# Forty series of five matmuls on one Trainium2 core behind the last product of a graph layer: weights from other tiles and at other strides, moving columns in other orders

## The reference, cut to what matters

```python
h = maximum(layernorm(x, axis=-1), 0.0)      # x: (4096, 256)
agg = matmul(adj, h)                         # adj: (4096, 4096)
out = x + relu(matmul(agg, W.T) + b)         # W: (256, 256), b: (256,)
```

## Time and profile before

| | us |
|---|---|
| device time, median of 2 runs | 382.73 (382.58 to 382.88) |
| device time of the profiled execution | 382.79 |
| span of the profiled execution, first to last instruction | 381.0 |
| TensorE busy with matmuls | 376.3 (99%) of 1649 matmuls |
| TensorE loading weights | 308.2 (81%), 1649 loads |
| DVE, ACT, POOL busy | 218.1, 170.9, 63.0 |

### The profile page before, as it was taken

How to read it: one execution, slowest core, us unless ns; L and a number is a source line. 1 busy time by engine, 2 the same in 40 slices (tenths; PEclk the granted TensorE clock), 3 DMA queues, 4 the chain that set the end, 5 groups by cost and what they waited for, 6 DMA issues and landing times.

```text
span 381.0 us, 4425 instructions
## 1 busy us (share of the span) xinstructions
PE 376.3 (99%) x1649; PEld 308.2 (81%) x1649; DVE 218.1 (57%) x293; ACT 170.9 (45%) x197; POOL 63.0 (17%) x79
## 2 busy tenths in 40 slices
PE   8999999999999999999999999999999999999996
PEld 4888888888888888888888888888888888888885
DVE  5999999994745353535564535353565344444424
ACT  4656655654553434343644343434364334343414
POOL 2787777760010000000001000000000100000000
PEclk9999999999999999999999999999999999999999
DMA  7987778669649565656565856565657675656203
GB/s 235 372 288 263 261 267 268 209 201 321 204 156 348 175 214 175 209 179 209 175 207 184 312 178 210 177 211 173 212 174 209 239 255 181 210 181 205 68 2 110
DMA packets 23062, 80.25 MB, mean 211 GB/s; under 512 B 2496, under 2 KB 3264, under 8 KB 23040
## 3 DMA queue, kind: packets, MB, share of 16 engines
q1 hardware_dynamic: 21024, 72.36, 58.0%
q0 software_dynamic: 2016, 7.60, 5.5%
HBM read 75.76 MB, written 4.19 MB: 210 GB/s over the span
## 4 chain that ended last, share of the span: by engine, by line
PE 99%; DVE 0%; ACT 0%; issue 0%
PE bank L379 92%; PE bank L420 6%; PE bank L429 1%; ACT out_sb L355 0%; DVE out_sb L292 0%; DVE warm L256 0%
## 5 line engine op out<-in xcount | busy, mean ns | idle before, releaser
L379 PE MATMUL bank<-adj_hi,h_sb 128*128 128x512 f32 x1024 | 255.1, 390 | 0.0
L223 DVE TENSOR_TENSOR adj_lo<-adj_in,adj_hi 128x1024 fp32r<-128x1024 f32 x126 | 154.2, 1224 | 138.6 <-ACT adj_hi L313 138.5
L379 PEld LDWEIGHTS bank<-adj_hi,h_sb 128*128 128x128 f32 x1024 | 192.3, 188 | 40.7 <-ACT h_sb L323 0.9
L313 ACT ACTIVATE adj_hi<-adj_in 128x1024 fp32r<-128x1024 f32 x126 | 133.4, 1059 | 160.7 <-PE bank L379 157.4
L379 PE MATMUL bank<-adj_lo,h_sb 128*128 128x512 f32 x512 | 137.9, 389 | 0.0
L379 PEld LDWEIGHTS bank<-adj_lo,h_sb 128*128 128x128 f32 x512 | 96.0, 188 | 20.5 <-DVE adj_lo L228 0.6
L203 POOL TENSOR_TENSOR rstd<-var_eps,minus_half 128x1 f32<-128x1 f32 x32 | 49.5, 1546 | 2.5
L215 POOL DMA_DIRECT2D out_t_dram<-out_sb x3 | 2.2, 723 | 209.7 <-DVE out_sb L292 209.7
L323 ACT ACTIVATE h_sb<-centred,rstd 128x256 fp32r<-128x256 f32 x32 | 16.3, 509 | 24.2 <-POOL rstd L203 24.0
L292 DVE TENSOR_TENSOR out_sb<-out_sb,xt_sb 128x512 f32<-128x512 f32 (+1 forms) x17 | 11.1, 659 | 7.7 <-ACT out_sb L355 7.7
L355 ACT ACTIVATE out_sb<-bank,b_sb 128x512 f32<-128x512 f32 (+1 forms) x17 | 11.3, 664 | 9.2 <-PE bank L420 9.2
(11 more groups left out here) (20 smaller groups left out, 31.6 us busy)
## 6 DMA issues: line engine op xcount, KB each, us to landing
adj_in<-adj_t_dram SPq DMA_DIRECT2D x126, 512.0 KB, 3.8
xt_sb<-x_t_dram POOLq DMA_DIRECT2D x4, 1024.0 KB, 7.2
x_sb<-x_dram SPq DMA_DIRECT2D x7, 512.0 KB, 6.5
out_t_dram<-out_sb POOLq DMA_DIRECT2D x3, 1024.0 KB, 5.0
adj_in<-adj_t_dram SPq DMA_DIRECT2D x4, 256.0 KB, 4.3
out_t_dram<-out_sb SPq DMA_DIRECT2D x3, 256.0 KB, 2.0
x_sb<-x_dram SPq DMA_DIRECT2D x4, 128.0 KB, 4.4
w_sb<-w_t_dram POOLq DMA_DIRECT2D x1, 256.0 KB, 5.2
```

The costliest lines, as they stand in the source:

```text
L223: nc.vector.tensor_tensor(adj_lo[:, k, :], adj_in[:, k, :], adj_hi[:, k, :].bitcast(fp32), ALU.subtract).then_inc(s_lo, 1)
L313: nc.scalar.activation(adj_hi[:, k, :], adj_in[:, k, :], ACT.Copy).then_inc(s_hi, 1)
L379: last = nc.tensor.matmul(bank(g, kb, c)[:], h_sb[:, t, hp, kb * P:(kb + 1) * P], adj_parts[ap][:, n % U, chunk(c)], start=(t == 0 and (hp ...
```

## The change: what it does

Behind `w_product(LAST)`, at the end of TensorE's program, `probes()` issues 40 series. Each calls `probe`, that is `REPEAT` = 5 identical matmuls of 128x512 with `start=True, stop=True`, which write `banks[0]` and `banks[1]` by turns. Nobody reads these banks afterwards, and there is no wait and no semaphore on these matmuls. Unless it is said otherwise, a series has 512 contiguous columns of `adj_hi` slot 0 as moving data.

- 5 series: weights from `h_sb`, tiles 0, 1, 2, 16, 31.
- 4 series: weights from `adj_lo` slot 2, beginning at element 0, 64, 128, 256.
- 2 series: weights of tile 0, moving data from `adj_hi` slots 1 and 2.
- 10 series: weights from `h_sb` read flat, with a step of 1 or 2 elements, from element 0, 4, 8, 16, 32; the moving columns run backwards, and so do the columns of the output.
- 15 series: weights with steps of 6, 14, 30, 62, 126 elements, from element 0, 8, 32.
- 1 series: weights with a step of 64.
- 3 series: weights of tile 0, moving data in runs of 8, 16 or 32 elements out of every 16, 32 or 64.

```diff
+            REPEAT = 5
+            t = TILES - 1
+
+            def probe(weights, moving=adj_hi[:, 0, 0:BANK], backwards=False):
+                for i in range(REPEAT):
+                    out = banks[i % 2][:]
+                    nc.tensor.matmul(out[:, ::-1] if backwards else out, weights, moving,
+                                     start=True, stop=True)
+
+            def runs(part, slot, size, length, at):
+
+                return part[:, slot, 0:2 * size].rearrange("p (r l) -> p r l", l=2 * length)[:, :, at:at + length]
+
+            h_flat = h_sb.rearrange("p t k d -> p (t k d)")
+
+            def probes():
+                for tile in (0, 1, 2, 16, 31):
+                    probe(h_sb[:, tile, 0, 0:P])
+                for at in (0, 64, 128, 256):
+                    probe(adj_lo[:, 2, at:at + P])
+                probe(h_sb[:, 0, 0, 0:P], adj_hi[:, 1, 0:BANK])
+                probe(h_sb[:, 0, 0, 0:P], adj_hi[:, 2, 0:BANK])
+                for step in (1, 2):
+                    for at in (0, 4, 8, 16, 32):
+                        probe(h_flat[:, at:at + (P - 1) * step + 1:step], adj_hi[:, 0, BANK - 1::-1], True)
+                for step in (6, 14, 30, 62, 126):
+                    for at in (0, 8, 32):
+                        probe(h_flat[:, at:at + (P - 1) * step + 1:step])
+                probe(h_flat[:, 0:(P - 1) * 64 + 1:64])
+                for length in (8, 16, 32):
+                    probe(h_sb[:, 0, 0, 0:P], runs(adj_hi, 0, BANK, length, 0))
...
             w_product(LAST)
+            probes()
```

## The result

The changed kernel takes 426.82 us (426.71 to 426.93) against 382.73 before, 1.115 times as long (95% interval 1.113 to 1.117). 425.9 was predicted.

The account below looks back on a forecast made before the run. TensorE bounds the kernel, busy 376.3 of 381.0 us. Start 377.37 plus 46.33 for 200 pitches plus 0.16 gives 423.86; handshake 0.25 makes the span 424.1, and 1.8 device time 425.9 us; range 422.9 to 436.0.

Parts of the forecast that it names:

- That everything adds up behind 377.3: End of TensorE's program: 200 new matmuls start at 377.37, only 3.6 us hidden, and their pitches add 46.33 us.
- rival D: New matmuls at the end run on unseen or are missing, so the time stays at 382.8 us; chance 0.02.
- Kind (a): 50 new matmuls with operands placed as in the main loop: 226.7 ns each, 11.3 us.
- (b): The other 150 new matmuls (`adj_lo` at 64, backward, strided weights, runs): 233 ns each as in the W product, 35.0 us.
- An even stream but for one series of five: Sign in the trace: first 45 new matmuls evenly spaced, except the five with `adj_lo` weights at element 64.
- The reason given, the place: Ground for 233 ns on unseen combinations: in the W product, too, only the place of the operands has changed.
- Rival B: The 50 matmuls with backward columns run at half rate, 427 ns each: 9.7 us more, 435.6 us; chance 0.13.
- Rival C: Many of the 150 unseen combinations cost only 213 ns: 32.0 instead of 35.0 us, 422.9 us; chance 0.07.
- For the strided weights the term: The 80 new matmuls with weight steps of 6 and more: 0.233 us each, 18.7 us.
- I keep 233 because the load has 227 - 118 = 109 ns of room: Strided weight loads could become nearly twice as slow and stay hidden under a 512-column matmul.
- Rival A: Strided loads disturb the moving stream: 293 ns for 80 matmuls, 430.7 us, or fully exposed 439.3; chance 0.20.
- That loads take nothing from the running matmul: Skill's rule, quoted but not adopted: weight loads take no SBUF bandwidth, 216 ns a matmul, 43.2 us for all 200.

Follow-up runs that it names:

- section 4: Changed kernel with its new series replaced by ones varying places of weights and moving data: 226.7 ns at the best places, W weights 233, bf16 215.9.
- section 1: Changed kernel with its new series replaced by 21 of 20 matmuls, weight steps 1 to 126, 512 then 256 columns: step 30 takes 249 and 244 ns.
- the second experiment: Changed kernel with its new series replaced by ones of 64, 96 or 128 weight columns: at step 30 and few moving columns, 126, 187 and 244 ns.

## Why the prediction was right

**That everything adds up behind 377.3.** Right. The first new matmul starts at 377.31 by the stretches, 377.37 was predicted, and the 0.06 us are those by which all of TensorE's pieces start earlier; 3.6 us of way out are hidden; the handshake waits for TensorE, which ends rival D. The span came out at 424.9 against 424.1.

**Kind (a), 226.7 ns.** Right: with the series at 64 elements, which the prediction put into (b), 12.53 us for 55, where 50 x 226.7 + 5 x 233.3 is 12.50. That series ran at 226.7, because 256 bytes change nothing. "An even stream but for one series of five" was wrong: the uneven ones are the first ten matmuls. They follow the halved products, but such beginnings also stand behind series of another place (section 4), and their cause is open.

**Kind (b), 233 ns.** Right for the backward columns: 11.67 us predicted and measured. The reason given, the place, fits eight of the ten series, which cost 230 to 233 ns forward too; at elements 0 and 4 with step 1 it is direction, for which the prediction had no reason, so that the right number there is luck. Rival B is refuted: 233 in place of 427 ns. Something near its price, 453 ns, is paid for a step of 2 of the moving data, which the change doesn't contain. Rival C did not come either: of the 150, only the series of `adj_lo` at 64 elements (227 ns) and that of step 64 (232) came below 233, and none came to 213.

For the strided weights the term was mis-sized: 80 x 233 = 18.7 us predicted, 18.30 + 1.16 = 19.46 measured. The step that failed is "I keep 233 because the load has 227 - 118 = 109 ns of room". That room is the room of a contiguous load. A load at a step of 4 and more uses all of it: 223 to 244 ns by the runs with 256 columns. The term came out only 0.8 us short because a scattered load of 128 columns happens to take about as long as 512 moving columns. Under 256 columns the same judgement would have been wrong by a factor of two, 244 against 120 ns. Rival A had the right place, and in the main the wrong mechanism and size: at steps of 14 and more (but for 64) the load outlasts the stream, and the pitch is 242 to 249 and not 293 ns. What is left of A's disturbance is the 6 to 9 ns of section 1.

The 15 with runs cost 236.6 in place of 233 ns, 0.05 us. Together 0.8 and 0.05, less the 0.06 us of the earlier start, give the 0.8 us by which the span exceeds 424.1; the other 0.1 us by which 426.82 exceeds 425.9 lies between the profiled execution, 426.71, and the median.

**That loads take nothing from the running matmul.** For bf16 the 216 ns that the prediction quotes from the Trainium skill ("TensorE: Matmul & The Clock Gate", section "Back-to-back issue gap") are what this chip does (215.9). For fp32r no pair of places in the runs settled below 226.7, and the excess depends on the distance of the two operands. That the two readings get in each other's way is the likely account; which resource they would share was not tried.

## What to carry to other kernels

Behind the last result, TensorE's work costs its full pitch, whether anybody reads it or not. Read the pitch from starts, not from the recorded length, and check a load's own time under a narrow matmul before calling it hidden: in fp32r, 128 weights that are 4 or more elements apart take 223 to 244 ns. Keep moving data in runs of at least 4 elements, and place weights and moving data a multiple of 256 bytes apart: that took 6.6 ns off each of 90 matmuls here for nothing.

## What was not expected of the hardware

- Moving float32 columns 2 elements apart take 453 ns for 512, steps of 4 and 8 take 461 and 431, runs of 4 take 233.
- A load of 128 weights at step 30 takes 244 ns at a granted clock of 0.50 as at 1.00.
- The granted clock reads 1.00 for the warm-up's matmuls, which come every 0.43 us, yet it reads 0.50 in the second experiment; the column of the first microseconds should be checked against the pitch.
